# One 512-column operand for the second layer of a mixture-of-experts block on one Trainium2 core

## What is computed

```python
x = x + _L0_gnn_ref(_layernorm(x), edge_weight, src, dst)     # x is 12500 x 256
x = x + _L0_ffn_ref(_layernorm(x)[None], gamma, beta, Wr, br, W1, b1, W2, b2)[0]
# inside _L0_ffn_ref: 8 experts, the best 2 for each row, D = 256, H = 512
logits = xn @ Wr + br;  top_vals, top_idx = top_k(logits, 2);  w = softmax(top_vals)
for e in range(8):
    h = gelu(xn @ W1[e] + b1[e])          # 256 -> 512
    y_e = h @ W2[e] + b2[e]               # 512 -> 256
    y = y + y_e * w_full[..., e, None]
```

## Time and profile before

| what | value |
|---|---|
| median of 3 runs | 1053.37 us (1051.1 to 1055.52) |
| the profiled execution | 1051.4 us, of which the trace's span is 1049.7 us |
| mean granted TensorE clock | 0.918 of full speed; 1.00 from 460 to 960 us |
| busy in the span | PE 87%, PEld 83%, DVE 72%, ACT 60%, POOL 58% |
| second stage | first matmul of `down` at 392.4 us, last at 1028.3 us |

### The profile page before, as it was taken

How to read it: one execution, slowest core, us unless ns; L and a number is a source line. 1 busy time by engine, 2 the same in 40 slices (tenths; PEclk the granted TensorE clock), 3 DMA queues, 4 the chain that set the end, 5 groups by cost and what they waited for, 6 DMA issues and landing times. The chain is left out here.

```text
span 1049.7 us, 25505 instructions
## 1 busy us (share of the span) xinstructions
PE 915.4 (87%) x6852; PEld 867.7 (83%) x6853; DVE 752.6 (72%) x2340; ACT 627.5 (60%) x1317; POOL 607.5 (58%) x465
## 2 busy tenths in 40 slices
PE   3756898988885349999999999999999999999991
PEld 3425777777775349999999999999999999999991
DVE  5856899999975627777777777777777777777761
ACT  2214666666664126677677667767766776776661
POOL 3230377777777724475655655655666564656553
PEclk9888898989895569999999999999999999999996
DMA  6013667777747644465554554554555455545542
GB/s 180 1 36 93 174 205 241 217 233 228 230 148 236 191 135 74 83 94 86 91 90 78 88 94 83 81 91 84 86 83 94 80 86 89 91 81 85 94 65 30
DMA packets 96200, 121.45 MB, mean 116 GB/s; under 512 B 15240, under 2 KB 73776, under 8 KB 96028
## 3 DMA queue, kind: packets, MB, share of 16 engines
q0 software_dynamic: 39904, 53.56, 29.7%
q1 hardware_dynamic: 55944, 66.55, 22.2%
q10 hardware_dynamic: 308, 0.85, 0.3%
HBM read 51.93 MB, written 68.98 MB: 115 GB/s over the span
## 5 line engine op out<-in xcount | busy, mean ns | idle before, releaser
L587 POOL DMA_INDIRECT out_dram<-ysb,yid x210 | 385.1, 1834 | 279.8 <-ACT ysb L1411 129.2
L774 PE MATMUL psum<-xh,w1s 128*128 128x256 f32 x1680 | 312.0, 285 | 0.0
L774 PEld LDWEIGHTS psum<-xh,w1s 128*128 128x128 f32 x1680 | 257.9, 189 | 0.0
L571 POOL DMA_INDIRECT slots<-arena_z,pos x196 | 196.4, 1002 | 98.7 <-issue 58.8
L787 PE MATMUL psum<-w2h,hl 128*128 x840 | 237.6, 283 | 0.0
L787 PE MATMUL psum<-w2l,hh 128*128 x840 | 237.2, 282 | 0.0
L787 PE MATMUL psum<-w2h,hh 128*128 x840 | 236.2, 281 | 0.0
L774 PE MATMUL psum<-xl,w1s 128*128 128x256 f32 x840 | 235.6, 281 | 0.0
L1209 DVE TENSOR_TENSOR hl<-hact,hh 128x512 fp32r<-128x512 f32 x210 | 145.6, 693 | 89.5 <-ACT hh L1267 89.5
L1394 ACT ACTIVATE hact<-psum,b1T 128x256 f32<-128x256 f32 x420 | 175.0, 468 | 14.3 <-PE psum L774 2.7
L1267 ACT ACTIVATE xh<-psum 128x512 fp32r<-128x512 f32 x105 | 62.8, 598 | 197.7 <-PE psum L761 197.7
(11 more groups left out here) (192 smaller groups left out, 1101.4 us busy)
## 6 DMA issues: line engine op xcount, KB each, us to landing
zin<-slots SPq DMA_DIRECT2D x105, 260.0 KB
arena_x<-in_x_dram SPq DMA_DIRECT2D x14, 512.0 KB, 5.4
out_dram<-arena_s SPq DMA_DIRECT2D x14, 512.0 KB
arena_x<-in_x_dram SPq DMA_DIRECT2D x13, 384.0 KB, 4.7
out_dram<-arena_s SPq DMA_DIRECT2D x13, 384.0 KB
stage_all<-in_L_ffn_W_dram SPq DMA_DIRECT2D x19, 256.0 KB, 3.6
out_dram<-ysb,yid POOLq DMA_INDIRECT x210, 4.2
slots<-arena_z,pos POOLq DMA_INDIRECT x196
```

The costliest lines, as they stand in the source:

```text
L571: pool.indirect_dma_start(slots[:, :], bass.IndirectOffsetOnAxis(ap=pos[b][0:n, k, s:s + 1], axis=0), zg[b][0:n, s, :], None).then_inc(sen ...
L587: pool.indirect_dma_start(out[:, :], bass.IndirectOffsetOnAxis(ap=yid[u % MB][:, n:n + 1], axis=0), ysb[u % YB][:, n, :], None, compute_op ...
L774: last = nc.tensor.matmul(bank[2 + 2 * b + q][:, m * PAIR:(m + 1) * PAIR], w1s[b][:, w, k, hb * P:(hb + 1) * P], xs[b][:, k * PAIR:(k + 1) ...
```

## The change

W2 gets one tile, `w2`, in which the high and the low 256 columns of a block of H lie side by side; `w2h` and `w2l` are views of it. `down` now gives TensorE the 512 columns [high, low] against one block of `hh` (`both`), and the 256 high columns against `hl` (`rest`). The product with the low part thus lands in columns 256 to 511 of a bank, and each tile `n` of a pair has its own bank, `bank[6 + n]`, which is the same one for every pair. DVE adds the two halves: per tile first half plus b2, then that sum plus the second half. The copies that fill `w2` write with a stride.

```diff
-        w2h = sb("w2h", [P, E, KH, D], F32R)
-        w2l = sb("w2l", [P, E, KH, D], F32R)
+        w2 = sb("w2", [P, E, KH, 2, D], F32R)
+        w2h, w2l = w2[:, :, :, 0, :], w2[:, :, :, 1, :]
...
             def down(i, u, e):
                 j, b = UN * i + u, u % 2
-                wait_from(pe, y_added, j - 1)
+
+                def both(n, k):
+                    return nc.tensor.matmul(bank[6 + n], hh[b][:, k * PAIR + n * P:k * PAIR + (n + 1) * P],
+                                            w2[:, bass.ds(e, 1), k, :, :].rearrange("p a w d -> p (a w d)"), start=(k == 0), stop=(k == KH - 1))
+
+                def rest(n, k):
+                    nc.tensor.matmul(bank[6 + n][:, 0:D], hl[b][:, k * PAIR + n * P:k * PAIR + (n + 1) * P],
+                                     w2[:, bass.ds(e, 1), k, 0, :].rearrange("p a d -> p (a d)"), start=False, stop=False)
+
                 for n in range(2):
+                    wait_from(pe, y_added, 2 * (j - 1) + n + 1)
                     for k in range(KH):
                         if n == 0 and k % 2 == 0:
                             pe.wait_ge(hl_ready, 2 * j + k // 2 + 1)
-                        for hs, ws in ((hh[b], w2h), (hh[b], w2l), (hl[b], w2h)):
-                            last = nc.tensor.matmul(bank[6 + b][:, n * D:(n + 1) * D], hs[:, k * PAIR + n * P:k * PAIR + (n + 1) * P],
-                                                    ws[:, bass.ds(e, 1), k, :].rearrange("p a h -> p (a h)"),
-                                                    start=(k == 0 and ws is w2h and hs is hh[b]), stop=(k == KH - 1 and hs is hl[b]))
-                last.then_inc(y_mm, 1)
+                        if k < KH - 1:
+                            both(n, k)
+                            rest(n, k)
+                        else:
+                            rest(n, k)
+                            both(n, k).then_inc(y_mm, 1)
...
             def y_bias(i, u, e):
                 j, b = UN * i + u, u % 2
                 wait_from(dve, y_ready, 2 * (j - 1))
-                dve.wait_ge(y_mm, j + 1)
-                v.tensor_tensor(ysum[b][:, :].rearrange("p (n d) -> p n d", n=2), bank[6 + b].rearrange("p (n d) -> p n d", n=2),
-                                b2all[:, bass.ds(e, 1), :].to_broadcast([P, 2, D]), ALU.add).then_inc(y_added, 1)
+                for n in range(2):
+                    y = ysum[b][:, n * D:(n + 1) * D]
+                    dve.wait_ge(y_mm, 2 * j + n + 1)
+                    v.tensor_tensor(y, bank[6 + n][:, 0:D], b2all[:, bass.ds(e, 1), :].rearrange("p a d -> p (a d)"), ALU.add).then_inc(y_first, 1)
+                    dve.wait_ge(y_first, 2 * j + n + 1)
+                    v.tensor_tensor(y, y, bank[6 + n][:, D:2 * D], ALU.add).then_inc(y_added, 1)
...
-                wait_from(act, y_mm, j - 1)
+                wait_from(act, y_mm, 2 * (j - 1))
                 copy(hh[b][:, half], hact[q][:, :]).then_inc(hh_ready, 1)
 
             def y_scale(i, u):
                 j, b = UN * i + u, u % 2
-                act.wait_ge(y_added, j + 1)
                 act.wait_ge(meta_ready, j + 1)
                 for n in range(2):
+                    act.wait_ge(y_added, 2 * j + n + 1)
```

More of the change, by code:

```diff
@@ L353, in build @@
         y_mm = sem("y_mm")
+        y_first = sem("y_first")
         y_added = sem("y_added")
@@ L978, in low2 @@
                 dve.wait_ge(w2_high, n + 1)
-                v.tensor_tensor(w2l[:, e, 2 * k:2 * k + 2, :].rearrange("p k d -> p (k d)"), stage2[n % W2B],
-                                w2h[:, e, 2 * k:2 * k + 2, :].rearrange("p k d -> p (k d)").bitcast(F32), ALU.subtract).then_inc(w2_low, 1)
+                v.tensor_tensor(w2l[:, e, 2 * k:2 * k + 2, :], stage2[n % W2B].rearrange("p (k d) -> p k d", k=2),
+                                w2h[:, e, 2 * k:2 * k + 2, :].bitcast(F32), ALU.subtract).then_inc(w2_low, 1)
             def route(g, b, full=True):
@@ L1066, in low_late @@
                 if w == 2:
-                    v.tensor_tensor(w2l[:, e, 2 * k:2 * k + 2, :].rearrange("p k d -> p (k d)"), a,
-                                    w2h[:, e, 2 * k:2 * k + 2, :].rearrange("p k d -> p (k d)").bitcast(F32), ALU.subtract).then_inc(late_low, 1)
+                    v.tensor_tensor(w2l[:, e, 2 * k:2 * k + 2, :], a.rearrange("p (k d) -> p k d", k=2),
+                                    w2h[:, e, 2 * k:2 * k + 2, :].bitcast(F32), ALU.subtract).then_inc(late_low, 1)
                 else:
@@ L1294, in high2 @@
                 act.wait_ge(stage2_in[n % W2B], 16 * (n // W2B) + 16)
-                copy(w2h[:, e, 2 * k:2 * k + 2, :].rearrange("p k d -> p (k d)"), stage2[n % W2B]).then_inc(w2_high, 1)
+                copy(w2h[:, e, 2 * k:2 * k + 2, :], stage2[n % W2B].rearrange("p (k d) -> p k d", k=2)).then_inc(w2_high, 1)
             def high_late(m):
@@ L1300, in high_late @@
                 if w == 2:
-                    copy(w2h[:, e, 2 * k:2 * k + 2, :].rearrange("p k d -> p (k d)"), a).then_inc(late_high, 1)
+                    copy(w2h[:, e, 2 * k:2 * k + 2, :], a.rearrange("p (k d) -> p k d", k=2)).then_inc(late_high, 1)
                 else:
```

## The result

The changed kernel takes 1047.01 us (median of 8 runs, 1045.75 to 1048.8), the kernel before 1050.96 us in the same comparison (8 runs). The ratio is 0.9956 with a 95% interval of 0.9940 to 0.9973: it is faster, by 0.44% or 4.6 us (the two medians lie 3.95 us apart), where 17.5 us were forecast. The time lies just above the range's upper end of 1046.

A forecast was written before the change was run, and what follows sets the result against it. PE's matmuls at full clock were taken to bound the second stage; 102 pairs x 0.172 us gave 17.5 us off 1051.4, 1033.9 us, stated as a median of 1035 us, range 1026 to 1046.

The forecast's parts named there:

- What bounds: Second stage: PE is busy throughout at full clock, so a pair costs its 52 matmuls; other engines have air.
- Part 1: PE in `down`: wide matmuls at 216 ns hide the weight load, narrow ones stay at 118.8; 172 ns less a pair.
- The narrow one with `hl` at 118.8: PE in `down`: the 256-column matmul stays at 118.8 ns, its stream too short to hide the next weight load.
- The fixed fee: Rival, PE in `down`: the 12 ns stay on every matmul; 96 ns less a pair, 1043.6 us; 10%.
- columns alone: Rival, PE in `down`: distance follows columns only; 0 to 2 us off, 1051 to 1053 us; 8%.
- Part 2: DVE, second stage: four additions replace one, +977 ns busy a pair, 91% of a step, hidden by the order.
- The slower rival: DVE, second stage: dearer additions make it the pace, step 6.28 us, 17 us added, 1071 us; 5%.
- Part 3: PE in `down`: new wait for the previous pair's `y_added`, slack 2.4 us or more, priced at 0.
- Parts 4 and 5: ACT, POOL, SP and first stage cost 0; at the end chained scatters lose the last three pairs' saving, 102 count.

The follow-up runs named there:

- m1_widths: Computation left out: rows of equal matmuls in several widths and formats, alone and beside other engines; float32r 512 columns start every 227 ns, 256 every 120.
- m3_runs: Computation left out: float32r matmuls alone, long runs of one width, then 512 and 256 columns mixed; 512 columns 226.7 ns in long runs, 230.1 to 233.2 mixed.
- m2_pattern: Computation left out: the exact matmul sequence of `down`, wide and narrow, alone and beside other engines; a pass takes 2826 ns wide, 2880 ns narrow.
- e1_narrow: Changed kernel with each 512-column matmul cut into two of 256 again, layout, banks and DVE's four additions kept; 1052.47 us, ratio 1.0002 to the kernel before.
- e2_one_add: Changed kernel without the second of each tile's two DVE additions, TensorE's work kept; 1046.12 us, ratio 0.9944 to the kernel before.

## Why the prediction was wrong

- **What bounds (right).** PE without a gap at full clock, before and after; the gain is what `down` loses in length, times the pairs.
- **Part 1, the price of a wide matmul (wrong, the step that failed).** "I price it at 213.3 + 2.5 = 216 ns." It is 233.0 in the kernel. Eight times the 17 ns are 136 of the 172 ns forecast. What is left is 36 ns; `down` before had 2860 ns over all pairs and not the 2850 of the one step read, which makes it the 46 measured. The 12 ns over the stream were read as a weight load that a longer stream would hide ("columns plus 2 ns and hides its weight load completely"). The reading rested on the plain float32 rows. In m1_widths plain float32 shows two such rows for each matmul, so they are passes and not matmuls, and their 2 ns were carried over to another format without a row that allowed it. The one float32r width in the trace could not tell a load from a fee. The excess over the columns is 13.3 ns in a long run (m1_widths, m3_runs) and 17 to 22 ns on a wide matmul in a mix (m3_runs, the kernel, m2_pattern).
- **The sum with the measured prices.** Eight matmuls fewer at 13.3 ns are 107 ns. Eight wide ones 6.3 ns dearer than in a long run take 50 back, eight narrow ones 1.4 ns cheaper than 120.0 give 11: 68, where e1_narrow and the changed kernel differ by 67. Against the kernel before it is 46, since its narrow ones stood at 119.2 and not at 120.0.
- **The narrow one with `hl` at 118.8 (right).** 116 to 122 ns, mean 118.6. The reason given for it holds in part at most: alone, half the block takes a 256-column distance from 120.0 to 113.3 ns (m1_widths), so the load is in it, but with about half of the 13.3 ns.
- **The rivals.** The fixed fee (225.5 ns, 96 ns a pair, 10%) came nearest in kind and missed the 6 ns of the mix; columns alone (237 ns, no change, 8%) came as near by number, but in a long run the slope is one column a cycle. The measured 46 ns lie between the two. The range ended at 1046 although a rival with 8% stood at 1051 to 1053.
- **Luck.** That the time lies only 1 us above the range is luck in part. The range was set from a median before of 1053.4 us (3 runs); the 8 runs give 1050.96, and a range set from that would have ended 2.4 us lower. The forecast's own sum, 1053.4 - 17.5, is 1035.9 and was written down as 1035.
- **Part 2, DVE (right).** 83 us in 100 where 91 were estimated: 0.98 us of durations were added to a busy time in which neighbours overlap. `h_low` still waits for ACT (65.9 us in 164 waits between 400 and 1000 us). Undoing the second addition gave nothing (e2_one_add). The slower rival fell.
- **Part 3, PE's wait (right).** 0.7 us in one wait.
- **Parts 4 and 5 (right).** The first `down` starts at 392.8 us (392.4 before). The last scatters after the change are 7.55, 6.71 and 6.54 us apart, where the earlier trace rows had 7.46, 7.01 and 6.58, so mainly the earlier pairs' saving shows: the first of them starts 4.28 us earlier, the span ends 4.5 earlier.

```profile
1011.84 2.12 POOL L588 DMA_INDIRECT out_dram<-ysb,yid  x1 [2.10 <-ACT ysb L1425]
...
1019.39 1.56 POOL L588 DMA_INDIRECT out_dram<-ysb,yid  x1 [3.56 <-issue]
...
1026.10 1.56 POOL L588 DMA_INDIRECT out_dram<-ysb,yid  x1 [3.28 <-ACT ysb L1425]
...
1032.64 1.56 POOL L588 DMA_INDIRECT out_dram<-ysb,yid  x1 [3.11 <-DMA out_dram<-ysb,yid]
```

What stays open: why a float32r matmul carries the 13 ns (at 256 columns half of it goes with half the stationary block, at 512 none does, and at 448 columns it is 20), and why the distance of a wide one depends on its neighbours (224 to 241 ns by place). The runs speak against the other engines, register addresses, the choice of bank and, for 512 columns, the load of a large block as causes.

## What to carry to other kernels

Merging two matmuls into one of the same columns saves at most the excess that each start has over its columns, so measure that excess in the format that is used, before counting on it: the distance between starts at two widths, and in the mix in which the kernel will run them. Here the long runs promised 107 ns a pair and the mix left 67. A distance at one width can't be split into columns and excess, and in this case another format's split didn't carry over. Additional work on an engine with a quarter of its time free was free here, and one run without it shows that.

## What the runs showed of the hardware

- Float32r matmuls in a long run at full clock, stationary block 128 x 128, start every 120.0, 146.7, 173.3 and 226.7 ns at 256, 320, 384 and 512 columns: one column a cycle at 2.4 GHz plus 13.3 ns. At 448 columns it is 206.7 ns, 20 over the columns, and at 128 and 192 columns 111.7. Bfloat16 has 109 and 216 ns at 256 and 512 columns, 2.5 over the columns; plain float32 is recorded as two passes a matmul, each of 216 and 429 ns (m1_widths, m3_runs).
- With a stationary block of 64 columns it is 113.3 ns at 256 columns, and at 512 columns 224 to 236, mean 230, without becoming steady (m1_widths).
- A row of 48 512-column float32r matmuls begins with two to nine distances of 224 to 236 ns and then stands at 227. Mixed with 256 columns most of them stand at 228 to 241 ns (all at 224 to 241; means from 230 to 236), while the 256-column ones get shorter (means from 115 to 119 in place of 120).
- DVE additions and copies between SBUF tiles, ACT reads of PSUM and loads from HBM, singly or (the copies left out) together, left the steady distance of 227 ns where it was, within 1 ns (m1_widths, m2_pattern).
- 24 narrow matmuls written to two banks, from the joint W2 tile and with the last block's order changed, stood 0.8 ns further apart (120.0 against 119.2 ns, e1_narrow), with one wait of PE for DVE in the stage (0.5 us).
